# Layer 0's product table on TensorE: whole-array products against products on 64 rows of the array, issued in pairs

## The reference, cut to what matters

```python
s1 = einsum('ea,eb,abc->ec',   xs, es, W1) / sqrt(64*8)       # 64 x 8 x 64
s2 = einsum('eai,ebi,abc->ec', xv, ev, W2) / (sqrt(3)*sqrt(32*8))
v1 = einsum('ea,ebi,abc->eci', xs, ev, W3) / sqrt(64*8)
v2 = einsum('eai,eb,abc->eci', xv, es, W4) / sqrt(32*8)
messages = concat((s1+s2)/sqrt(2), (v1+v2)/sqrt(2)) @ Wm + bm
agg      = segment_sum(messages, src)
x        = layernorm(x + x + concat(x, agg) @ Wu + bu)
```

## Time and profile before

| | |
|---|---|
| median of three runs | 2801.99 us (2800.79 to 2812.91) |
| span of the profiled execution | 2803.6 us, 1.6 us above the median |
| TensorE products busy | 2524.3 us (90%) |
| TensorE weight loads busy | 2222.2 us (79%) |
| VectorE, GpSimd, ScalarE busy | 70%, 59%, 39% |
| `front_phase` | from 0 to about 1263 us |
| granted TensorE clock, mean | 0.975 |

### The profile page before, as it was taken

How to read it: one execution, slowest core, us unless ns; L and a number is a source line. 1 busy time by engine, 2 the same in 40 slices (tenths; PEclk the granted TensorE clock), 3 DMA queues, 4 the chain that set the end, 5 groups by cost and what they waited for, 6 DMA issues and landing times. The chain is left out here.

```text
span 2803.6 us, 54254 instructions
## 1 busy us (share of the span) xinstructions
PE 2524.3 (90%) x15994; PEld 2222.2 (79%) x15994; DVE 1956.9 (70%) x5468; ACT 1083.7 (39%) x2711; POOL 1662.3 (59%) x1770
## 2 busy tenths in 40 slices
PE   3999999999999999995999959999999999999997
PEld 1777777777777777785999959888888888888886
DVE  7777667766667677654877757776766676667766
ACT  2665566666666666651222212222222222222221
POOL 1666566666666666661001027777777777777775
PEclk8999999999999999997999979999999999999999
DMA  7899999999989898955888844333333333333332
GB/s 226 261 318 316 290 309 317 317 320 317 286 288 289 282 296 286 293 185 200 293 288 281 295 143 123 87 88 88 100 88 88 87 99 88 88 87 100 89 87 68
DMA packets 424477, 571.17 MB, mean 204 GB/s; under 512 B 72616, under 2 KB 369273, under 8 KB 411594
## 3 DMA queue, kind: packets, MB, share of 16 engines
q10 hardware_dynamic: 237795, 282.85, 31.3%
q0 software_dynamic: 84144, 149.09, 18.5%
q1 hardware_dynamic: 102248, 135.62, 15.2%
HBM read 339.23 MB, written 228.11 MB: 202 GB/s over the span
## 5 line engine op out<-in xcount | busy, mean ns | idle before, releaser
L448 POOL DMA_INDIRECT placed<-message,slots_now x784 | 764.8, 976 | 459.7 <-ACT message L624 277.8
L1468 POOL DMA_INDIRECT f_y<-y_table,b_rec x894 | 853.5, 955 | 289.0 <-issue 177.7
L533 PEld LDWEIGHTS g_bank<-quad_ring,front_work 128*128 128x128 f32 x4704 | 663.5, 191 | 175.2 <-issue 172.7
L533 PE MATMUL g_bank<-quad_ring,front_work 128*128 x4704 | 737.0, 307 | 66.7 <-issue 51.6
L807 DVE SCALAR_TENSOR_TENSOR front_work<-g_bank,quarter_node,front_work 128x512 f32<-128x512 f32 x588 | 404.5, 743 | 138.9 <-issue 61.6
L1658 PE MATMUL e_bank<-f_msg,f_hot 128*126 128x160 f32 x1788 | 387.7, 312 | 74.7 <-DVE f_msg L1532 73.3
L1529 DVE TENSOR_TENSOR f_msg<-e_bank,f_y 128x256 f32<-128x256 f32 x447 | 189.0, 423 | 317.5 <-issue 207.6
L1653 PE MATMUL e_bank<-f_msg,f_hot 128*126 128x160 f32 x1788 | 395.5, 303 | 16.2 <-DVE f_msg L1532 12.4
L1658 PEld LDWEIGHTS e_bank<-f_msg,f_hot 128*126 128x126 f32 x1788 | 281.9, 190 | 126.6 <-DVE f_msg L1532 125.9
L613 ACT COPY front_work<-front_work 32x512 f32<-32x512 f32 x588 | 362.4, 616 | 23.1 <-issue 8.5
L1641 PE MATMUL e_bank<-fc,b_hidden 100*128 100x192 f32 x1788 | 371.0, 330 | 0.0
(11 more groups left out here) (253 smaller groups left out, 2894.9 us busy)
## 6 DMA issues: line engine op xcount, KB each, us to landing
products<-g ACTq DMA_DIRECT2D x49, 2560.0 KB, 9.9
quad_ring<-products ACTq DMA_DIRECT2D x98, 1280.0 KB
big<-placed SPq DMA_DIRECT2D x49, 1458.0 KB, 7.0
b_lengths<-length_parts ACTq DMA_DIRECT2D x447, 45.0 KB
placed<-zeros SPq DMA_DIRECT2D x24, 648.0 KB
f_y<-y_table,b_rec POOLq DMA_INDIRECT x894
front_work<-in_e_t SPq DMA_DIRECT2D x196, 64.0 KB
placed<-message,slots_now POOLq DMA_INDIRECT x784, 7.8
```

Source lines behind the costliest of these rows:

```text
L448: pool.indirect_dma_start(v.placed[:, :], bass.IndirectOffsetOnAxis(slots_now[tile // SET % SLOT_SETS][:, tile % SET:tile % SET + 1], 0), ...
L533: pe.matmul(bank_now[:, n * D:n * D + D], spread[batch % SPREADS][:, j, q * P:q * P + P], ring[:, bass.ds(slot + j, 1), :].rearrange("p a ...
L1468: pool.indirect_dma_start(f_y[:, tile % Y_RING, :], None, v.y_table[:, :], bass.IndirectOffsetOnAxis(b_rec[b % REC_RING][:, j, 0:1], 0)).t ...
```

## The change

Each product uses only the 64 rows of the array that hold its features. The units' order is changed, so that upper rows (0 to 63) and lower rows (64 to 127) take turns: unit 0 is `one` (upper), unit 1 `two` (lower), unit 2 `four` (now loaded to rows 0 to 31, upper, with a copy of W2 in a new tile `wc`), unit 3 `three` (lower); unit 4 is `one` and `four` (both upper), unit 5 `two` and `three` (both lower). Two units are issued together behind pairs 0, 2 and 4, in place of one behind each of pairs 0 to 5. ScalarE still takes one unit a pair. Two more weight loads go on ScalarE's queue, VectorE clears rows 32 to 63 of `wc`, waits for nine loads in place of seven and scales two more pieces.

```diff
+        wa, wb, wc = sb("w_first", [P, 512]), sb("w_second", [P, 256]), sb("w_upper", [S, 768])
...
+                act.dma_start(wc[0:V, 0:512], t["w2"]).then_inc(first_loads, 16)
+                act.dma_start(wc[0:V, 512:768], t["w4"]).then_inc(first_loads, 16)
...
-                dve.wait_ge(first_loads, 16 * 7)
+                dve.memset(wc[V:S, :], 0.0)
+                dve.wait_ge(first_loads, 16 * 9)
...
-                for weight, k in ((wa[0:S, :], K1), (wa[S:P, :], K2), (wb[0:S, :], K3), (wb[S:P, :], K4)):
+                for weight, k in ((wa[0:S, :], K1), (wa[S:P, :], K2), (wb[0:S, :], K3), (wb[S:P, :], K4), (wc[0:V, 0:512], K2), (wc[0:V, 512:768], K4)):
...
-                    sp.dma_start(four[64:96, :], t["x_t"][128:160, at]).then_inc(x_in[b % 2], 16)
+                    sp.dma_start(four[0:32, :], t["x_t"][128:160, at]).then_inc(x_in[b % 2], 16)
...
-                    if j < 4:
-                        last = pe.matmul(into[:], xs[j][:], wa[:], start=True, stop=True)
+                    upper, lower = slice(0, S), slice(S, P)
+                    if j == 0:
+                        last = pe.matmul(into[:], one[upper, :], wa[upper, :], start=True, stop=True)
+                    elif j == 1:
+                        last = pe.matmul(into[:], two[lower, :], wa[lower, :], start=True, stop=True)
+                    elif j == 2:
+                        last = pe.matmul(into[:], four[upper, :], wc[:, 0:512], start=True, stop=True)
+                    elif j == 3:
+                        last = pe.matmul(into[:], three[lower, :], wa[lower, :], start=True, stop=True)
+                    elif j == 4:
+                        pe.matmul(into[:, 0:256], one[upper, :], wb[upper, :], start=True, stop=True)
+                        last = pe.matmul(into[:, 256:512], four[upper, :], wc[:, 512:768], start=True, stop=True)
                     else:
-                        m = 2 * (j - 4)
-                        pe.matmul(into[:, 0:256], xs[m][:], wb[:], start=True, stop=True)
-                        last = pe.matmul(into[:, 256:512], xs[m + 1][:], wb[:], start=True, stop=True)
+                        pe.matmul(into[:, 0:256], two[lower, :], wb[lower, :], start=True, stop=True)
+                        last = pe.matmul(into[:, 256:512], three[lower, :], wb[lower, :], start=True, stop=True)
...
                 def produce(i, k):
-                    if k < PARTS6:
+                    if k % 2 == 0 and k < PARTS6:
                         unit(i + LEAD, k)
+                        unit(i + LEAD, k + 1)
                     elif k == PARTS6:
                         rank(i + LEAD)
```

More of the change, by code:

```diff
@@ L240, in front_phase @@
         slots_now = [sb(f"slots_now{g}", [P, SET], I32) for g in range(SLOT_SETS)]
-        wa, wb = sb("w_first", [P, 512]), sb("w_second", [P, 256])
+        wa, wb, wc = sb("w_first", [P, 512]), sb("w_second", [P, 256]), sb("w_upper", [S, 768])
         alone = [[sb(f"x_alone{k}{m}", [P, P]) for m in range(4)] for k in range(2)]
@@ L478, in unit @@
                     n = b * PARTS6 + j
-                    xs, into = alone[b % 2], p_unit[n % 2]
+                    one, two, three, four = alone[b % 2]
+                    into = p_unit[n % 2]
                     if j == 0:
@@ L583, in take_unit @@
                     if j < 4:
-                        last = act.copy(into[:, 8 * j:8 * j + 8, 0:S], full[:].rearrange("p (b c) -> p b c", c=S))
+                        m = (0, 1, 3, 2)[j]
+                        last = act.copy(into[:, 8 * m:8 * m + 8, 0:S], full[:].rearrange("p (b c) -> p b c", c=S))
                     elif j == 4:
@@ L587, in take_unit @@
                             act.copy(into[:, 8 + 8 * c:16 + 8 * c, S + 32 * c:S + 32 * c + 32], eight[:, 0, :, :])
-                        last = act.copy(into[:, 0:8, S:S + 32], eight[:, 1, :, :])
+                        last = act.copy(into[:, 0:8, S + 64:S + 96], eight[:, 1, :, :])
                     else:
-                        act.copy(into[:, 0:8, S + 32:S + 64], eight[:, 0, :, :])
-                        last = act.copy(into[:, 0:8, S + 64:S + 96], eight[:, 1, :, :])
+                        act.copy(into[:, 0:8, S:S + 32], eight[:, 0, :, :])
+                        last = act.copy(into[:, 0:8, S + 32:S + 64], eight[:, 1, :, :])
                     last.then_inc(units_taken, 1)
```

## The result

The changed kernel takes 2839.07 us, the median of four runs (2837.59 to 2847.43), against 2803.93 us for the kernel before in the same comparison (2800.79 to 2812.91): 1.013 times, with a 95% interval of 1.0108 to 1.0152. It is slower by more than the 0.5% that a measurement can tell. The forecast said 2810 us and a change too small to be told (0.44), against 0.40 for slower; 2839 lies in its range of 2782 to 2844, near the upper end, though not for the reasons that had set that end.

What follows compares the result with a forecast made beforehand. PE was taken to bound the kernel, busy 90% of the span. Blocks -4 us, late evictions +11 and start +1 gave +8: 2811.6 us for the profiled execution, so 2810 us, range 2782 to 2844.

Steps and rivals of the forecast that it cites:

- The block: Eight pairs between two like rows on PE: 24.14 us forecast, 0.08 less than 24.22; -4 us over 46 blocks.
- Stretch 1 to 3: PE from pair 1's row to pair 3's: 6.25 us against 6.03, as unit 3 waits for unit 1's eviction.
- the bubble: PE's idle gap behind unit 0, ahead of pair 1: 1.24 us a block, in which unit 1 would hide.
- rival B: Ahead of pair 1: the word load slips 0.38 us, giving +26 us, 2828; chance 0.22.
- B's slip of 0.21 us: Ahead of pair 1: the word load's slip from which the slower rival with that load was said to decide.
- the three slots of 0.43: Units 2 and 3: partial overlap in issue order, three product slots in place of four, 1.29 us.
- C: Couples of units: the halves do not run side by side; stretch 1 to 3 becomes 6.43 us, total 2819; chance 0.20.
- Stretch 3 to 5: PE from pair 3's row to pair 5's: 6.60 us against 6.04, the word load standing behind unit 5's waiting load.
- D: Word load goes ahead of waiting unit 5 (6.22 us) and late evictions are absorbed: -20 us, 2782; chance 0.20.
- the late evictions: Every fifth block, at the ring's wrap: unit 3 waits 1.2 us for unit 1's eviction; nine blocks, +11 us (0 to 18).
- The two changes of rows: Around each pair of units between whole-array products: 0.19 to 0.20 us a change, 0.39 us a pair of units.
- the start: Ahead of the loop: extra weight loads cost some 2 us, overlap saves about 1; +1 us (-2 to +3).

Runs made afterwards that it cites:

- x2: The changed kernel with one unit behind each of pairs 0 to 5, as before, on half the rows: 3264.34 us, 1.005 of the kernel before.
- x1: The kernel before with units issued two together behind pairs 0, 2 and 4, products still on all 128 rows: 3283.48 us, 1.010.
- x4: The kernel before with ScalarE's eviction of a unit ahead of the features' copies and the ring's load: 3198.56 us, 0.9969.
- x13: The changed kernel with two units together behind pairs 0, 3 and 5, and the store issued behind the ring's load: 3227.71 us, 1.0066 of the kernel before.
- a2: The changed kernel measured again, unedited, on another chip: 3246.62 us, 1.0117 of the kernel before.
- x10: The changed kernel with only the ring's load moved behind the eviction of the same pair: 3249.55 us, 1.0119 of the kernel before.
- x12: The kernel before with units issued two together on the whole array and the ring's load behind the evictions: 3243.13 us, 1.0107.

## Why the prediction came out as it did

**Right: what is saved is not on the path.** The block was given 24.14 us against 24.22; outside the late pairs the loop is 4.6 us shorter than before, against -4. The usual block did not get shorter, though: the median of the blocks that are not late is 24.23 us after and 24.24 before. The 4.6 us are in their means (24.50 and 24.66), and what they come from is not shown. Stretch 1 to 3 is 6.24 for 6.25. Unit 1 hid in the bubble, and the word load ahead of pair 1 did not slip (pair 0 to 1 4.14 us for 4.10), so rival B fell. (B's slip of 0.21 us, from which it decides, was worked out wrong: it takes the saving of 0.08 us a block off twice. From +8 us to 14 it needs 6 / 46 = 0.13 us. Nothing else hangs on it.) The load behind a waiting weight load does start behind it: the one ahead of pair 3 in the late block starts at 618.9, with L496.

**Right in the sum, wrong in the parts.** Products side by side overlap wholly, 0.86 us a couple, not in the three slots of 0.43 that I took; C fell too. Stretch 3 to 5 has a median of 6.70 us for 6.60, but by another way, so the agreement is luck: pair 5 often has its couple without a wait (3.17 us behind pair 4, as from 674.90 on in the block above), and pair 4 waits for the ring's load (median 3.17 us in place of 2.42; PE's waits for that load rose from 14.7 to 28.4 us). So what unit 5 gained was given back at pair 4. D fell with that, and because no pause absorbed the late evictions. The two changes of rows were priced 0.20 each from products on 32 rows, and x2 shows 0.20 for 64.

**The step that failed: the late evictions, +11 us.** The nine blocks were the right ones and the cause was the right one. I sized the wait by one block, whose eviction came 4.63 us after its row. It was the lowest of the nine in that trace, which reach 5.97 with a mean of 5.25; after the change they are 5.02 to 6.47, mean 5.57, since the wrap's issue was longer too (on average 7.16 us for 6.85). Against the ordinary 3.41 that makes the wait 2.2 us where I had 1.2. To this comes what was in no term: 3.41 us at half clock behind each wait, of which 0.7 us are lost ahead of pair 3's row in the block shown and up to 1.6 in others. By the rows the waits make 19.5 us and what follows them 11.2. Measured 31 us for 11, of which the upper end had 18. The text had said that it would be wrong if the clock fell in these windows; it fell in every fifth.

**The other term mis-sized: the start, +1 us.** It was +4.9. I had let the overlap save 1 us there, and it costs: units that end together are evicted in a burst with TensorE idle, at half speed throughout.

4.9 + 26.7 + 1.5 make the 33.1 us of the two spans; the forecast had 8.

**Luck.** That 2839 lies in the range is luck. The upper end of 2844 was B and C together, with late evictions at 18 us and the start at 2. B and C both fell, and the late evictions and the start each went beyond what that end had for them; two terms that were too small came out near the sum of two rivals that did not happen. The likeliest outcome of the three, a change too small to be told, did not come.

The forecast cited "TensorEngine Tiling (Array Packing)" of the Trainium skill, "PSUM Bottleneck": tiling does not make evacuation faster, and evacuation may become the bottleneck. The traces agree that evictions cost the time, with 1.0117 falling to 1.0011 when only the order on ScalarE changes. They do not agree that tiling brought it about: x1 has 77 us of waits for evictions with every product on the whole array, more than the changed kernel, so what made the evictions count was that two units are issued together.

**Open.** Why x4 gains 0.3%, and why x13 does not come under the kernel before. The half clock was not taken away by itself, so its share of a late block (11 of 31 us) rests on the rows, not on a run. That the wrap at pair 7 starts each late block rests on ten issues and nine late blocks that follow them, on the first chip and again in a2, x1, x10 and x12 (30.3 to 30.5 us, against 26.0 to 26.4 in the others); neither edit aimed at it removed it cleanly.

## What to carry to other kernels

When two uses of a double buffer are moved together, the second one waits for the emptying of the buffer's last use: look up when that ends after every kind of block, the worst included, not in one block. And ask what the engine that empties it does in order ahead of it; here a new order on it was worth 1% (0.3% in the kernel that had no such waits to speak of), and products side by side nothing. If a transfer is moved later, look at what stands behind it in its queue.

## What the runs showed of the hardware that I had not expected

Products on disjoint halves of the array start 6 to 13 ns apart, and not in the order of the program. In the block shown, to the nanosecond, L490 starts at 661.075, L492 at 661.082, L490's second product at 661.609 and L492's second at 661.615; the program has both of L490 ahead of both of L492. "TensorE: Matmul & The Clock Gate" of the Trainium skill, Part 3, says that such products run together but start in the order of the program. The first half agrees with these rows, the second does not: the later unit's first product is 527 ns ahead of the earlier unit's second. Units 0 and 1 are one matmul each, of two products, so there one could still say that the matmuls kept their order. Units 4 and 5 are two matmuls each, in the program L498, L499, L501, L502, and in the same block L501 starts ahead of L499:

```profile
675.26 0.48 PE L498 MATMUL g_bank<-w_second,x_alone 64*128 64x256 f32 x1
675.28 0.48 PE L501 MATMUL g_bank<-w_second,x_alone 64*128 64x256 f32 x1
...
675.80 0.38 PE L499 MATMUL g_bank<-w_upper,x_alone 64*128 64x256 f32 x1
675.81 0.38 PE L502 MATMUL g_bank<-w_second,x_alone 64*128 64x256 f32 x1
```

Where unit 5 comes late, the order is that of the program (in a2 L499 starts at 1301.42 and L501 at 1301.84).

A wait of TensorE can cost more than its own length. The wait ahead of pair 3 in the late blocks (1.71 us of idle products in the one shown, 2.54 of the weight load) was followed in nine of nine cases by a stretch of 3.41 us at 1.2 GHz, while it was busy again; over the nine the waits cost 19.5 us and the slower products behind them 11.2. In the start of the changed kernel the products run at half speed up to the first pair, where those of the kernel before were at full speed by 51 us (two of 256 columns in 0.43 us, 51.55 to 51.98), and at half again at its first pair.
